# Another order and other banks for all pieces of a two-layer transformer kernel

## The reference

```python
# layer 0, once per batch
h = layernorm(x)
q, k = rope(split(h @ Wq.T + bq)), rope(split(h @ Wk.T + bk))
att = softmax(causal(q @ k.T / 4.0)) @ split(h @ Wv.T + bv)
x1 = x + layernorm(att @ Wo.T + bo)
h = layernorm(x1)
x2 = x1 + layernorm((gelu(h @ Wgate.T) * (h @ Wup.T)) @ Wdown.T)
# layer 1
h = layernorm(x2)
s = 50 * tanh(q1 @ k1.T / 8.0 / 50)
x3 = x2 + layernorm(softmax(causal(s)) @ v1 @ Wo1.T)
h = layernorm(x3)
out = x3 + layernorm(sigmoid(xr @ Wr.T) * (relu(xk @ Wk.T) ** 2 @ Wv.T))
```

## Time and profile before

| | us |
|---|---|
| median of 3 runs | 1564.12 |
| lowest and highest | 1562.08, 1564.25 |
| the profiled execution | 1562.13 |
| span of its profile | 1560.4 |
| around the span | 1.73 |
| PE busy | 1450.1 (93%) |
| VectorE busy | 1153.0 (74%) |
| GpSimd busy | 831.5 (53%) |
| ScalarE busy | 799.7 (51%) |
| mean granted clock of TensorE | 0.965 |

### The profile page before, as it was taken

One profiled execution on the slowest core, in us unless ns is written; L12 is line 12 of the kernel. 1 busy time (PEld: TensorE's weight loads), 2 busy tenths in 40 slices (PEclk: granted clock), 3 DMA queues, 4 the chain that ended last, 5 costly groups with the idle time before them and its releaser, 6 DMA issues.

```text
span 1560.4 us, 29738 instructions
## 1 busy us (share of the span) xinstructions
PE 1450.1 (93%) x10854; PEld 1062.3 (68%) x10854; DVE 1153.0 (74%) x1844; ACT 799.7 (51%) x1132; POOL 831.5 (53%) x1003
## 2 busy tenths in 40 slices
PE   4878989899999997999999999999999999999997
PEld 3546666676666666677776776777767777767765
DVE  5679697878788886766657668778697687874875
ACT  2344344353435343645665656556566566565651
POOL 4143445353535453436656666566676565756652
PEclk9679999999999998999999999999999999999998
DMA  7341333333333335101100010100101001000000
GB/s 171 67 63 25 56 77 47 69 55 68 54 68 54 68 41 122 41 29 42 56 7 1 1 41 1 41 1 1 40 0 36 5 0 40 0 0 28 1 28 14
DMA packets 47268, 60.84 MB, mean 39 GB/s; under 512 B 5296, under 2 KB 32848, under 8 KB 47184
## 3 DMA queue, kind: packets, MB, share of 16 engines
q1 hardware_dynamic: 46320, 59.03, 18.5%
q10 hardware_dynamic: 864, 0.66, 0.1%
HBM read 25.83 MB, written 8.39 MB: 22 GB/s over the span
## 4 chain that ended last, share of the span: by engine, by line
PE 47%; POOL 17%; issue 16%; DVE 11%; DMA 4%; ACT 3%; SPq 2%; POOLq 0%; ACTq 0%; DVEq 0%
PE psum L422 23%; PE psum L1968 4%; POOL l_probs L301 4%; PE psum L1933 4%; POOL l_keysum L1602 4%; PE psum L1194 3%; POOL l_keysum L1604 3%; PE psum L1164 3%; PE psum L1984 2%; POOL l_attT_lo L1610 2%; DVE l_rowmax L979 2%; PE psum L1118 2%; DMA l_qT<-l_roped_hi 2%; DVE l_att L1759 2%; PE psum L1956 2%
## 5 line engine op out<-in xcount | busy, mean ns | idle before, releaser
L1675 ACT ACTIVATE l_probs<-psum 128x1024 f32<-128x1024 f32 (+1 forms) x192 | 164.0, 879 | 168.1 <-PE psum L1933 151.8
L1759 DVE RECIPROCAL l_att<-psum 128x512 f32<-128x512 f32 x64 | 214.5, 3352 | 47.9 <-PE psum L1956 39.8
L897 ACT ACTIVATE l_probs<-psum 128x512 f32<-128x512 f32 x256 | 138.2, 594 | 168.6 <-PE psum L1164 160.7
L979 DVE TENSOR_REDUCE l_rowmax<-psum 128x2 f32<-128x1024 f32 (+2 forms) x192 | 159.4, 862 | 48.2 <-PE psum L1125 47.9
L301 POOL TENSOR_SCALAR_AFFINE_SELECT l_probs<-l_probs 128x256 f32<-128x256 f32 (+1 forms) x384 | 186.8, 520 | 0.0
L1681 ACT ACTIVATE l_probs<-l_probs 128x2048 f32<-128x2048 f32 (+1 forms) x128 | 160.6, 1267 | 0.8
L1750 DVE TENSOR_TENSOR l_qk_lo<-psum,l_qk_hi 128x1024 fp32r<-128x1024 f32 x64 | 77.2, 1212 | 112.2 <-ACT l_qk_hi L1665 112.1
L1968 PE MATMUL psum<-l_probs,l_v 128*64 128x512 f32 (+3 forms) x1024 | 150.5, 436 | 1.0 <-DVE l_att L1765 1.0
L296 POOL TENSOR_TENSOR l_pool_holder<-expo 128x1 f32<-128x1 f32 x128 | 31.6, 247 | 186.7 <-ACT l_probs L1681 118.2
L1968 PEld LDWEIGHTS psum<-l_probs,l_v 128*64 128x64 f32 x1024 | 70.4, 137 | 88.5 <-issue 78.5
L410 POOL TENSOR_TENSOR l_x_rstd<-l_x_veps,expo 128x4 f32<-128x4 f32 (+1 forms) x50 | 53.2, 1064 | 140.7 <-DVE l_x_veps L403 140.6
(11 more groups left out here) (210 smaller groups left out, 4175.9 us busy)
## 6 DMA issues: line engine op xcount, KB each, us to landing
l_kT<-l_roped_hi SPq DMA_DIRECT2D x64, 128.0 KB, 4.2
l_qT<-l_roped_hi SPq DMA_DIRECT2D x64, 128.0 KB, 5.1
l_xin<-in_x SPq DMA_DIRECT2D x8, 512.0 KB, 4.1
l_kT<-l_roped_lo SPq DMA_DIRECT2D x32, 128.0 KB, 5.2
l_qT<-l_roped_lo SPq DMA_DIRECT2D x32, 128.0 KB, 5.0
l_x<-in_x SPq DMA_DIRECT2D x8, 512.0 KB, 4.0
x_mid<-l_x SPq DMA_DIRECT2D x8, 512.0 KB, 3.0
l_xin<-x_mid SPq DMA_DIRECT2D x8, 512.0 KB, 4.9
```

The source lines that it names most:

```text
L897: space.free(nc.scalar.activation(probs[:, SLOT[p], e, c0:c1], space.unit(*use), ACT.Exp, scale=HD0 ** -0.5), *use)
L979: reduced = nc.vector.tensor_reduce(rowmax[:, a // 2, :, a % 2, t], space.unit("max", a, k)[:, :, c0:c0 + (t + 1) * P], mybir.AxisListType ...
L1675: space.free(nc.scalar.activation(probs[:, p % 2, :, c0:c1], space.unit("score", p, u)[:, :, 0:c1 - c0], ACT.Tanh, scale=HD1 ** -0.5 / CLA ...
L1759: space.free(nc.vector.reciprocal(att[p % 2][:], space.unit("den", p)), "den", p)
```

## The change

Every due time in the tables of both layers is replaced, with the times of the first and last rounds and of the loads. Most of the new numbers keep the order; some pieces change sides with neighbours. Before the loop 68 of PE's 225 pieces stand elsewhere (VectorE 44 of 173, ScalarE 32 of 125, GpSimd 12 of 70, SyncE 5 of 33). In layer 0's looped round it is 8 of 82 on PE, 9 of 48 on ScalarE, 11 of 64 on VectorE, 8 of 27 on GpSimd and 1 of 11 on SyncE; at the seam 9 of 33 on SyncE. No instruction is added or removed. Banks: `maxT` (1) goes from 3 to 1, `score` (4, 0) unit 0 from 4 to 5, `outT` (2) from 4 to 5, and most unread products go to other banks.

The diff has nearly 290 changed lines on each side, all in tables; these are the lines the text speaks of. Where a long line is cut, only its changed entries stand here.

```diff
     table = {
...
-        "rope": {(0,): -8.85, (1,): -6.86, (2,): -0.77, (3,): 5.27},
+        "rope": {(0,): -8.95, (1,): -6.65, (2,): -0.87, (3,): 5.39},
...
-        "rope_lo": {(0,): -6.92, (1,): -4.1, (2,): 3.46, (3,): 6.47},
+        "rope_lo": {(0,): -9.21, (1,): -5.2, (2,): 5.54, (3,): 7.06},
...
-        "place": {(0,): 1.92, (1,): 9.15, (2,): 16.42, (3,): 17.53},
+        "place": {(0,): 6.04, (1,): 9.99, (2,): 13.7, (3,): 15.72},
...
-        "score": {(0, 0): 7.67, (0, 1): 8.61, (1, 0): 12.13, (1, 1): 14.05, (2, 0): 14.44, (2, 1): 16.04, (3, 0): 16.75, (3, 1): 17.84, (4, 0): 20.19, (4, 1): 20.7, (5, 0): 23.53, (5, 1): 25.98, (6, 0): 27.92, (6, 1): 29.64, (7, 0): 30.36, (7, 1): 31.2},
+        "score": {(0, 0): 7.73, (0, 1): 8.44, (1, 0): 11.93, (1, 1): 13.96, (2, 0): 14.51, (2, 1): 16.03, (3, 0): 16.73, (3, 1): 17.351, (4, 0): 19.84, (4, 1): 20.73, (5, 0): 23.21, (5, 1): 25.75, (6, 0): 28.51, (6, 1): 29.7, (7, 0): 30.02, (7, 1): 31.21},
...
-        "exp": {(0, 0): 9.44, (0, 1): 9.6, (1, 0): 16.13, (1, 1): 16.21, (2, 0): 16.76, (2, 1): 17.89, (3, 0): 19.08, (3, 1): 20.41, (4, 0): 22.38, (4, 1): 22.97, (5, 0): 27.35, (5, 1): 27.9, (6, 0): 29.7, (6, 1): 30.56, (7, 0): 31.05, (7, 1): 33.42},
+        "exp": {(0, 0): 9.821, (0, 1): 9.89, (1, 0): 14.12, (1, 1): 16.46, (2, 0): 16.54, (2, 1): 18.29, (3, 0): 18.41, (3, 1): 19.96, (4, 0): 21.81, (4, 1): 21.89, (5, 0): 26.44, (5, 1): 28.81, (6, 0): 29.58, (6, 1): 31.22, (7, 0): 31.78, (7, 1): 33.76},
...
-        "mask": {(0,): 8.92, (1,): 10.92, (2,): 13.92, (3,): 17.45, (4,): 21.07, (5,): 24.91, (6,): 29.58, (7,): 29.82},
+        "mask": {(0,): 9.33, (1,): 10.55, (2,): 15.39, (3,): 18.44, (4,): 23.02, (5,): 26.19, (6,): 27.47, (7,): 29.84},
...
-        "max": {(0, 0): 2.31, (0, 1): 3.12, (1, 0): 3.69, (1, 1): 4.05, (2, 0): 6.471, (2, 1): 7.51, (3, 0): 7.73, (3, 1): 8.88, (4, 0): 13.38, (4, 1): 14.18, (5, 0): 15.1, (5, 1): 16.17, (6, 0): 18.88, (6, 1): 20.29, (7, 0): 20.74, (7, 1): 21.38},
+        "max": {(0, 0): 2.11, (0, 1): 3.44, (1, 0): 3.91, (1, 1): 4.52, (2, 0): 6.33, (2, 1): 7.24, (3, 0): 7.86, (3, 1): 8.76, (4, 0): 13.14, (4, 1): 14.44, (5, 0): 15.7, (5, 1): 16.07, (6, 0): 17.62, (6, 1): 20.26, (7, 0): 21.05, (7, 1): 21.1},
...
-        "maxT": {(0,): 6.78, (1,): 12.031, (2,): 18.41, (3,): 25.43},
+        "maxT": {(0,): 7, (1,): 12.34, (2,): 18.18, (3,): 25.33},
...
-        "maxT_out": {(0,): 8, (1,): 13.44, (2,): 20.04, (3,): 27.37},
+        "maxT_out": {(0,): 8.31, (1,): 13.141, (2,): 19.94, (3,): 27.1},
...
-        "maxima": {(0,): 12.68, (1,): 20.66, (2,): 24.69, (3,): 35.25},
+        "maxima": {(0,): 13.68, (1,): 18.441, (2,): 24.66, (3,): 35.1},
...
-        "tail": {(0,): 13.29, (1,): 18.93, (2,): 27, (3,): 31.241},
+        "tail": {(0,): 12.96, (1,): 19.11, (2,): 27.43, (3,): 31.221},
...
-        "exp_tail": {(0,): 15.51, (1,): 21.02, (2,): 29.261, (3,): 32.12},
+        "exp_tail": {(0,): 15.721, (1,): 21.13, (2,): 29.241, (3,): 32.37},
...
-        "tanh": {(0,): 45.42, (1,): 47.14, (2,): 48.97, (3,): 50.67, (4,): 53.21, (5,): 53.44},
+        "tanh": {(0,): 44.661, (1,): 46.24, (2,): 50.73, (3,): 51.051, (4,): 53.24, (5,): 53.35},
...
-        "x1_T": {(0,): 40.61, (1,): 41.76},
+        "x1_T": {(0,): 40.9, (1,): 41.21},
...
-        "residual": {(): 42.28},
+        "residual": {(): 39.81},
...
-        "x2_rstd": {(): 54.86},
+        "x2_rstd": {(): 54.6},
...
-        "x2": {(): 56.6},
+        "x2": {(): 55.33},
...
-        "store": {(): 66.03},
+        "store": {(): 63.74},
...
-        "max_tail": {(0,): 5.67, (1,): 10.35, (2,): 16.59, (3,): 22.4},
+        "max_tail": {(0,): 5.68, (1,): 10.44, (2,): 16.66, (3,): 22.66},
...
     moved_table = {
...
         "maxima": {
...
-(0, 7): 199.42,
+(0, 7): 193.92,
...
-(1, 7): 217.03,
+(1, 7): 209.64,
...
-(2, 7): 228.33,
+(2, 7): 225.62,
...
-(3, 7): 234.5,
+(3, 7): 231.12,
         "residual": {
...
-(6,): 209.02,
+(6,): 210.68,
...
-(7,): 240.28,
+(7,): 242.72,
         "store": {
...
-(5,): 206.3,
+(5,): 204.72,
...
-(6,): 239.7,
+(6,): 236.11,
...
-(7,): 263.47,
+(7,): 288.36,
...
     bank_table = {
...
-        "maxT": {(0,): 7, (1,): 3, (2,): 3, (3,): 7},
+        "maxT": {(0,): 7, (1,): 1, (2,): 3, (3,): 7},
...
-        "outT": {(0,): 2, (1,): 1, (2,): 4, (3,): 1},
+        "outT": {(0,): 2, (1,): 1, (2,): 5, (3,): 1},
...
-        "warm": {(0,): 0, (1,): 1, (2,): 4, (3,): 7, (4,): 6, (5,): 6, (6,): 2, (7,): 6, (8,): 7, (9,): 7, (10,): 2, (11,): 5, (12,): 5, (13,): 6, (14,): 4, (15,): 3},
+        "warm": {(0,): 1, (1,): 5, (2,): 5, (3,): 1, (4,): 3, (5,): 3, (6,): 7, (7,): 6, (8,): 7, (9,): 2, (10,): 2, (11,): 4, (12,): 2, (13,): 7, (14,): 7, (15,): 2},
...
         "score": {
...
-(4, 0, 0): 4,
+(4, 0, 0): 5,
...
@@ layer 1 @@
     table = {
...
-        "o": {(0,): 14.76, (1,): 16.621, (2,): 23.992, (3,): 25.003, (4,): 27.124, (5,): 30.115, (6,): 33.686, (7,): 36.187},
+        "o": {(0,): 14.83, (1,): 16.771, (2,): 23.842, (3,): 25.563, (4,): 26.644, (5,): 30.665, (6,): 33.176, (7,): 36.407},
...
-        "tanh": {(0, 0): 5.44, (0, 1): 5.87, (0, 2): 7.2, (1, 0): 7.54, (1, 1): 7.97, (1, 2): 8.18, (2, 0): 10.29, (2, 1): 10.88, (2, 2): 10.98, (3, 0): 11.68, (3, 1): 12.54, (3, 2): 14.68, (4, 0): 15.63, (4, 1): 16.18, (4, 2): 16.62, (5, 0): 19.98, (5, 1): 20.1, (5, 2): 21.02, (6, 0): 24.47, (6, 1): 24.5, (6, 2): 26.01, (7, 0): 26.6, (7, 1): 27.17, (7, 2): 27.3},
+        "tanh": {(0, 0): 5.31, (0, 1): 5.83, (0, 2): 6.9, (1, 0): 7.69, (1, 1): 7.761, (1, 2): 7.86, (2, 0): 10.65, (2, 1): 10.78, (2, 2): 10.95, (3, 0): 11.33, (3, 1): 11.63, (3, 2): 14.85, (4, 0): 15.49, (4, 1): 16.06, (4, 2): 16.641, (5, 0): 19.98, (5, 1): 20.28, (5, 2): 20.91, (6, 0): 23.97, (6, 1): 24.09, (6, 2): 24.9, (7, 0): 25.71, (7, 1): 26.32, (7, 2): 27.73},
...
-        "exp": {(0, 0): 7.86, (0, 1): 8.26, (1, 0): 8.86, (1, 1): 9.78, (2, 0): 11.66, (2, 1): 11.661, (3, 0): 13.73, (3, 1): 15.05, (4, 0): 16.6, (4, 1): 18.18, (5, 0): 20.75, (5, 1): 22.57, (6, 0): 24.51, (6, 1): 26.67, (7, 0): 28.17, (7, 1): 28.65},
+        "exp": {(0, 0): 6.89, (0, 1): 8.22, (1, 0): 8.23, (1, 1): 10.09, (2, 0): 11.1, (2, 1): 11.31, (3, 0): 14.4, (3, 1): 15.22, (4, 0): 17.17, (4, 1): 17.98, (5, 0): 21.26, (5, 1): 22.76, (6, 0): 24.25, (6, 1): 26.6, (7, 0): 27.72, (7, 1): 28.7},
...
-        "att_hi": {(0,): 12.17, (1,): 13.71, (2,): 16.54, (3,): 20.59, (4,): 24.82, (5,): 28.96, (6,): 32.09, (7,): 32.55},
+        "att_hi": {(0,): 13.06, (1,): 14.86, (2,): 16.221, (3,): 20.76, (4,): 23.39, (5,): 29.15, (6,): 31.41, (7,): 33.22},
...
     moved_table = {
...
         "tanh": {
...
-(7, 0, 6): 418.61,
+(7, 0, 6): 417.402,
...
-(7, 1, 6): 419.33,
+(7, 1, 6): 417.74,
         "exp": {
...
-(6, 0, 6): 417.403,
+(6, 0, 6): 417.403,
...
-(6, 1, 6): 417.404,
+(6, 1, 6): 417.404,
...
-(7, 0, 6): 420.34,
+(7, 0, 6): 419.43,
         "att_hi": {
...
-(4, 6): 417.405,
...
-(5, 6): 420.15,
+(5, 6): 417.405,
         "o": {
...
-(4, 6): 418.675,
+(4, 6): 417.967,
         "score": {
...
-(7, 0, 6): 417.411,
+(7, 0, 6): 417.9,
...
-(7, 1, 6): 417.412,
+(7, 1, 6): 417.97,
...
-(7, 2, 6): 417.45,
+(7, 2, 6): 418.29,
...
     prologue_table = {
...
-        "load": {(0,): 221.86, (1,): 229.19, (2,): 214.44, (3,): 203.64, (4,): 236.55, (5,): 239.15, (6,): 255.24, (7,): 244.9, (8,): 274.95, (9,): 262.25},
+        "load": {(0,): 216.29, (1,): 220.73, (2,): 217.07, (3,): 210.95, (4,): 235.96, (5,): 231.98, (6,): 245.76, (7,): 253.01, (8,): 260.62, (9,): 259.44},
...
     bank_table = {
...
-        "end_heat": {(0,): 4, (1,): 0, (2,): 2, (3,): 5, (4,): 0, (5,): 4, (6,): 3, (7,): 1, (8,): 2},
+        "end_heat": {(0,): 4, (1,): 3, (2,): 3, (3,): 2, (4,): 3, (5,): 5, (6,): 1, (7,): 0, (8,): 2},
...
```

## The result

The changed kernel is slower: 1577.93 us (median, 1576.75 to 1578.80) against 1563.15 us of the kernel before, measured beside it, a ratio of 1.0095 with a 95% interval of 1.0079 to 1.0111. I had forecast 1558.5 us and a range of 1545 to 1570.

The account below looks back on a forecast made before the run. TensorE's matmuls bound the kernel, so only waits and clock could change. Terms -5.5 - 4.0 + 4 + 1 = -4.5 took the profiled 1562.13 us to 1557.6, 1559.6 in the median's terms; forecast 1558.5, range 1545 to 1570.

Parts of the forecast that it names:

- term 6: Head, end and unread products: many moves against neighbours, taken as 0, with one dip of +-4 us.
- Term 3: Layer 0's four looped rounds: new waits outweigh one removed, +1.0 us each, +4 in all; per-round bounds -0.7 and +3.
- the first rival: Layer 0's looped rounds: later place[3] delays store, residual and maxima, PE waits for DMA; about 1571 us, chance 0.22.
- the bank is given back: Layer 0's loop: tail[0] waits about 0.5 us for maxT's readout; a later wait gives back nearly all.
- The gain for the rotated queries: Layer 0's looped rounds: rope_lo[1] ahead of hidden_lo[0] on GpSimd removes PE's wait of 0.68 us.
- Term 4: Clock in layer 0's looped rounds: a dip in all four, at most 2 us each; +1 us, between -6 and +2.
- the sign turns: Layer 0's loop: from 2.4 us a round, clock included, the loss outweighs the 9.5 us gained at seam and layer 1.
- Term 1: Seam of the layers: SyncE issues maxima before residual, removing PE's 5.49 us wait; -5.5 us, bounds 8 and 3 us.
- Term 2: Start of layer 1's last round: tanh before the exponentials on ScalarE removes wait and dip; -4.0 us, bounds -2 and -5.
- Term 5: Layer 1's looped rounds: some eight matmul groups pass neighbours, 0 us; bounds -2 and +7 over seven or so rounds.

Follow-up runs that it names:

- seam_end: Kernel before with the change's order only at the seam and behind layer 1's loop, both loops and head old: 1552.65 us, 0.9946.
- rest_new: Kernel before with the change's order at the seam, in layer 1's loop and at the end: 1554.05 us, 0.9944.
- head_xnorm3: Kernel before with the change's order ahead of layer 0's loop, but batch 3's x_norm put back behind the low parts: 1569.0 us, 1.005.
- only_xnorm3: Kernel before with batch 3's x_norm alone moved ahead of the low parts on VectorE: 1564.09 us, 1.0003.
- only_rope3: Kernel before with rope_lo[3] alone moved behind x2_rstd on GpSimd in layer 0's loop: 1568.42 us, 1.0042.

## Why the prediction was wrong

Two steps failed and turned the sign: term 6, which has the head at 0, where it cost 8.3 us; and terms 3 and 4, which have layer 0's loop at +4 and its clock at +1, where the loop cost 14.0 us.

**Term 3 and the first rival, layer 0's loop: the chain right, its price too low.** Counted from the same transpose (432.47 before, 366.75 after), the trace shows the chain of the prediction nearly to the tenth:

| | before | predicted | after |
|---|---|---|---|
| place[3] issued | +6.4 | 4 later | +10.3 |
| store | +13.7 | +14.2 | +14.3 |
| residual | +16.8 | +19.6 | +19.8 |
| maxima | +20.2 | +20.4 | +20.2 |
| maxima usable by PE | | +23.9 | +24.4 |
| PE there | +22.8 | +22.9 | +22.5 |

(before's last entry: 375.33 less its wait of 0.30, less 352.25.) The wait was then put at 1.0 and is 1.87 us: 0.5 us because the copy takes 4.15 us from its issue, not 3.5 (it was issued 0.2 us sooner), and 0.4 us because PE comes earlier. The store took 5.3 us to land, as predicted (5.4), instead of 2.9. The rotary product's wait (1.11, put at 1.0 to 1.3) and that of tail[1] (1.00, put at about 1) are as predicted, and the bank is given back. PE's waits of over 0.15 us in the round sum to 6.9 us, and to 5.0 in the second round before: +1.9 us, where I had +1.0. Over the looped stretch PE stands 8.1 us more, where the term has +4. The error was to take 1.0 us for a wait whose own bounds were 0 and 2.6. The Trainium skill's rule on ring order ("DMA: Bandwidth & Descriptors", section "Queues, rings and completion order"), as the prediction quotes it, spoke for the upper part. The traces agree: the copy took 4.15 us from its issue with the load 0.46 us ahead of it, and no more than 2.8 us with the load 2.9 us ahead. The gain for the rotated queries (-0.7) was also claimed for a piece that does not bring it, and in every round, where the kernel before has the wait in two.

**Term 4, the clock in these rounds: the dip in all four came, its price did not.** The term allowed 1 us, between -6 and +2, because a dip was to cost 2 us at most. One more full dip (in the first round, 2.4 us of PE's busy time) and a full one in place of a half (the fourth) came to 3.6 us. Terms 3 and 4 together make 2.7 us a round, where the sum has 1.25. That is above the 2.4 us at which I had said the sign turns. I had the rival's mechanism, place and threshold and gave it 0.22; its price, 18 us for the four rounds, stands against 14.0 measured.

**Term 6, the head: a term put at nothing.** I put 0, with one dip of +-4, on 68 moved pieces of PE and 44 of VectorE, because nothing spoke for a sum. It cost +8.3 us by itself. The rows needed were in the trace: VectorE's normalization, GpSimd's addition and the low parts stood within 3 us of each other, and the order of the first against the last was in the diff. I did not go through the head as I had gone through the loop. The rows would have shown the new wait, not its price: this move alone costs the old kernel nothing that can be told, and in the changed kernel 6.8 of the 10.1 us that the stretch loses beside the moved work are the lower clock.

**Term 1, the seam: mechanism right, size wrong.** The maxima went at 607.59 (607.9 predicted), ahead of the residual, and the wait of 5.49 us is gone. The residual landed for VectorE at 613.33, as predicted. But the gain is 2.7 us in the trace (x1_T at 623.74 instead of 626.49; I had 621), of which 0.5 us stood already at 564.5 us, and 3.3 us in the runs, near the lower bound of 3. The next late thing was not only VectorE. PE waits 2.30 us for the tail's exponential on ScalarE, which I had not followed, and 0.80 us for another. And the clock gave nothing back, against the 2.0 us of the term: the half clock now lies at 614.4 to 621.3 us, where PE is busy for 6.71 us; before, at 611.8 to 622.1 us, it lay in good part under the long wait, and PE was busy for 4.82 us of it.

**Term 2: mechanism right, the number in part by luck.** The wait and the dip at 1403 are gone. In `seam_end`, with layer 1's old loop, the round that had them takes 102.88 us instead of 106.65: -3.8, where I had 4.0. In the changed kernel it takes 104.49, only 2.2 us less, because the new loop's wait of 1.37 us for `l_qk_lo` stands in it too. The other 2.0 us of its -4.3 lie between the last two transposes of line 1995 (67.60 us instead of 69.61), where I had forecast nothing.

**Term 5 was right** within what can be told of whole times: `seam_end` without and `rest_new` with the new loop are equal. Its sign, rounds no longer than before, failed by 0.2 us a round, and the new wait for `l_qk_lo` is one that I had not found.

**The sum.** Predicted: seam -5.5, layer 1 and the end -4.0, layer 0's loop with its clock +5, head 0. The runs: -3.3, -5.4, +14.0, +8.3. Left open is the rest of the head. The new last round is slow whatever precedes it and whichever of PE and VectorE keeps its old order. Batch 3's `x_norm` is worth 3.5 us of that stretch in `head_xnorm3`, but 7.8 us in the changed kernel (91.1 - 83.3) and 2.1 us in the old one. The time in which PE stands differs little between the three (1.5, 2.2 and 2.7 us); its busy time, which is the clock, differs by 2.0, 5.6 and -0.6 us. Why a dip follows in one and not in another, no run tells.

## What to carry to other kernels

Where pieces are reordered under a full TensorE, follow every queue that a late piece heads, down to the last small DMA behind it. One low part made later on an idle engine put a 512 KB load directly ahead of a small copy, and cost 6.6 us alone and 8.4 us in company. Price such a wait together with the dips of the clock that it adds, which here were more than half of its cost, and give "many small moves" a width from the density of waits around them, not zero. And split a reordering by stretch before judging it: its seam and end alone were worth 8 us, its loop and head cost 22.

## What the runs showed of the hardware

**VectorE waits for GpSimd.** Four normalizations of 128x256 (input and output in SBUF) took 1.37 us alone, 3.45 us where GpSimd's 128x1024 addition began 0.23 us after them, and 2.59 us where it had begun 0.92 us before. The addition took 2.38 to 2.43 us each time, in the kernel before too, where no normalization lay beside it. In the changed kernel VectorE's group ended 0.79 us after the addition (209.24 against 208.45), in `only_xnorm3` 1.12 us (207.86 against 206.74), about the time of two and of three of the four, which take 0.34 us each alone. That fits a VectorE that stood still until the addition had ended; GpSimd did not slow down. The Trainium skill, "SBUF — State Buffer", section "Who interferes with whom", says that VectorE and GpSimd share a pair of SBUF ports, that `tensor_scalar` can take it, and that who comes first holds it for the whole instruction while the other is blocked. The trace agrees: 2.08 us more beside an addition of 2.43 us, and 1.22 us more for the overlap of 1.47 us (206.74 - 205.27).

**A small copy behind a load.** The maxima's copy, issued 0.46 us behind the residual's 512 KB load, was usable by PE 4.1 us later in two kernels; issued 2.9 us behind it, it kept nobody waiting at 2.8 us (376.38 - 373.55).

**The first 200 us vary from run to run.** With the same order up to there the transpose came at 197.66 in one profiled execution and at 202.31 in another; PE was busy for 151.91 us up to there in the one and 157.48 in the other, so the clock makes the difference. Differences of whole times under 5 us in the head are told better by a stretch, whose own spread was 1.4 us, than by the end.

**What a short wait costs.** One piece moved alone (`only_rope3`) let PE stand 1.9 us more in the looped rounds and be busy 3.6 us more with the same matmuls, at a granted clock of 0.95 instead of 0.97.
